# Fused attention and feed-forward kernel: the quantised stage's two maxima by matrix product, its row factors computed inside the rotary block, its first unit by quarters

## The reference, cut to what matters

```python
x = x + _L0_xattn_ref(_layernorm(x), ctx, ctx, ...)      # rotary attention, out @ Wo
x = x + _L0_ffn_ref(_layernorm(x), clip_x, clip_down, w_gate, w_up, w_down)

def _act_fake_quant(x, clip_factor):
    scale = sigmoid(clip_factor) * max(abs(x)) / 127      # ONE scale for the whole tensor
    return clip(round(x / scale), -128, 127) * scale
def _weight_fake_quant(w):                                # one scale for each row
    scale = max(abs(w), axis=1) / 127
    return clip(round(w / scale), -128, 127) * scale
xq = _act_fake_quant(x, clip_x)
gate, up = xq @ wq(w_gate).T, xq @ wq(w_up).T             # 512 -> 1408
h = _act_fake_quant(silu(gate) * up, clip_down)
return h @ wq(w_down).T
```

## Time and profile before

| | us |
|---|---|
| median of 3 timed executions | 1569.18 |
| lowest and highest | 1568.81, 1569.34 |
| span of the profiled execution | 1565.3 |
| PE busy | 1471.0 (94%) |
| DVE busy | 1184.2 (76%) |
| ACT busy | 881.9 (56%) |
| POOL busy | 489.1 (31%) |

### The profile page before, as it was taken

How to read it: one execution, slowest core, us unless ns; L and a number is a source line. 1 busy time by engine, 2 the same in 40 slices (tenths; PEclk the granted TensorE clock), 3 DMA queues, 4 the chain that set the end, 5 groups by cost and what they waited for, 6 DMA issues and landing times. The chain is left out here.

```text
span 1565.3 us, 30701 instructions
## 1 busy us (share of the span) xinstructions
PE 1471.0 (94%) x10998; PEld 1078.9 (69%) x11022; DVE 1184.2 (76%) x2306; ACT 881.9 (56%) x2093; POOL 489.1 (31%) x436
## 2 busy tenths in 40 slices
PE   7899999999999999599998998999999977998997
PEld 5677777777777777444443467888888866776885
DVE  5677777886777655478878968888888756787875
ACT  3444444444444443456657838888988865664342
POOL 0122222222222221200002544545545434664333
PEclk9999999999999999799999999999999998999998
DMA  8411111110111101113304810000000007225641
GB/s 308 153 45 44 44 44 44 44 40 8 43 34 34 43 8 75 44 75 148 148 1 178 324 40 3 4 2 2 3 4 3 4 1 269 82 82 182 205 151 60
DMA packets 47808, 118.35 MB, mean 76 GB/s; under 512 B 9422, under 2 KB 15950, under 8 KB 46032
## 3 DMA queue, kind: packets, MB, share of 16 engines
q1 hardware_dynamic: 42016, 100.03, 18.1%
q0 software_dynamic: 5680, 16.85, 2.7%
HBM read 78.89 MB, written 39.80 MB: 76 GB/s over the span
## 5 line engine op out<-in xcount | busy, mean ns | idle before, releaser
L1721 ACT ACTIVATE c_probs<-c_score,c_minus_top 128x128 f32<-128x128 f32 x512 | 183.8, 422 | 2.0 <-DVE c_minus_top L1833 2.0
L1676 POOL TENSOR_TENSOR c_probs<-c_probs,c_recip 128x1024 f32<-128x1024 f32 x64 | 121.7, 1902 | 169.7 <-DVE c_recip L1839 169.7
L689 POOL TENSOR_TENSOR a_attn_lo_parts<-a_attn,a_attn_hi_parts 128x512 fp32r<-128x512 f32 x64 | 80.1, 1285 | 250.2 <-ACT a_attn_hi_parts L747 250.2
L1721 ACT ACTIVATION_READ_ACCUMULATOR c_probs<-c_score,c_minus_top 128x1 f32 x512 | 133.9, 262 | 0.0
L743 ACT COPY a_attn<-a_pv_ps 128x512 f32<-128x512 f32 x64 | 37.0, 578 | 162.7 <-PE a_pv_ps L998 162.6
L425 PE MATMUL a_bank<-a_x_hi_parts,a_wq_hi 128*128 128x256 f32 x512 | 106.8, 290 | 0.3 <-PEq L440 0.3
L2287 ACT CAST d_xT_hi<-d_turn 128x512 fp32r<-128x512 f32 x71 | 41.7, 587 | 110.1 <-PE d_turn L2531 103.1
L425 PE MATMUL a_bank<-a_x_lo_parts,a_wq_hi 128*128 128x256 f32 x512 | 103.0, 283 | 0.0
L425 PE MATMUL a_bank<-a_x_hi_parts,a_wq_lo 128*128 128x256 f32 x512 | 102.8, 282 | 0.0
L966 PE MATMUL a_bank<-a_wo_hi,a_attn_hi_parts 128*128 128x512 f32 x256 | 102.4, 400 | 0.0
L967 PE MATMUL a_bank<-a_wo_lo,a_attn_hi_parts 128*128 128x512 f32 x256 | 101.1, 395 | 0.0
(11 more groups left out here) (310 smaller groups left out, 4276.0 us busy)
## 6 DMA issues: line engine op xcount, KB each, us to landing
hidden<-b_hidden SPq DMA_DIRECT2D x5, 2816.0 KB, 8.1
b_hidden<-hidden SPq DMA_DIRECT2D x5, 2816.0 KB, 11.9
xres<-in_x SPq DMA_DIRECT2D x8, 1024.0 KB, 14.0
d_we<-in_we SPq DMA_DIRECT2D x8, 1024.0 KB, 12.7
xres<-in_w_gate_up SPq DMA_DIRECT2D x7, 1024.0 KB, 5.3
d_got<-rows SPq DMA_DIRECT2D x20, 258.0 KB, 2.9
xres<-rows SPq DMA_DIRECT2D x19, 258.0 KB, 2.9
a_rot<-in_rot SPq DMA_DIRECT2D x16, 256.0 KB, 3.1
```

The lines of the kernel that those rows point to most:

```text
L689: nc.gpsimd.tensor_tensor(of_spread(attn_lo, g), of_spread(attn, g), of_spread(attn_hi, g), ALU.subtract).then_inc(attn_lo_ready, 1)
L1676: nc.gpsimd.tensor_tensor(part, part, recip[:, t % 2, heads].unsqueeze(2).to_broadcast([P, HALF, KEYS]), ALU.mult).then_inc(scaled, 1)
L1721: last = nc.scalar.activation(probs[:, t, at, :], score_ps[:, h, g, :], ACT.Exp, bias=minus_top[:, h, g:g + 1], accum_out=total[:, t, at:a ...
```

## The change

1. **Both maxima by a product.** POOL's two reductions over partitions go. PE multiplies the column of 128 partition maxima, broadcast as the stationary operand, with the identity (one fp32 product of 128 columns). Each partition then holds all 128 values in PSUM, and DVE reduces them.
2. **Row factors inside the rotary block.** `center` of the last two tiles, the power, the sigmoid, the first maximum and the chain behind it move from the quantised stage's first block to the end of the rotary block. The sigmoid's two instructions come behind the aggregation of the first 30 tiles.
3. **Weights turned elsewhere.** 6 groups ahead of `output(0)` instead of 9, none of them waiting for ACT; the other 6 behind `output(1)`, still in the rotary block. ACT loads Silu's table ahead of its seventh copy. `output(0)` starts when two of the four low parts are there, and waits for the other two at its fifth block.
4. **Rows turned tile by tile.** In the first chunk PE turns tile t as soon as it is rounded, and ACT copies it.
5. **First unit by quarters.** Behind each tile but the first PE issues the gate and up products of the previous tile's 128 rows for unit 0; the usual loop leaves unit 0 out.
6. **Down weights.** SP no longer waits for the turned groups in this stage.

```diff
-    GROUPS_AHEAD = 9
+    GROUPS_AHEAD = 6
@@ rotary block, POOL, behind chunks(pool, body)
+                pool.wait_ge(ahead.var_ready, 2)
+                late = ahead.rstd[:, TILES - NT:]
+                nc.gpsimd.tensor_tensor(late, late, minus_half[:], ALU.pow).then_inc(ahead.rstd_ready, 1)
@@ ACT
-                for g in range(ahead.GROUPS_AHEAD):
+                for g in range(len(ahead.GROUPS)):
+                    if g == ahead.GROUPS_AHEAD:
+                        nc.scalar.activation(warm[:], minus_half[:, 0:1], ACT.Silu)
                     act.wait_ge(ahead.turned, g + 1)
@@ DVE, behind chunks(dve, body)
+                dve.wait_ge(ahead.seen_here, 2 * NT)
+                seen.center(nc, ahead_steps, ahead, slice(TILES - NT, TILES))
+                dve.wait_ge(ahead.rstd_ready, 2)
...
+                nc.vector.tensor_reduce(peak, seen.top[:], AX.X, ALU.max).then_inc(ahead.peak_ready, 1)
+                dve.wait_ge(ahead.peak_turned, 1)
+                ahead_steps.step(nc.vector.tensor_reduce(x_scale, peak_bank[:, 0, 0:P], AX.X, ALU.max))
...
+                nc.vector.scalar_tensor_tensor(ahead.shift[:], ahead.mv[:, :, 0], -1.0, ahead.rstd[:], ALU.mult, ALU.mult)
+                nc.vector.tensor_scalar(ahead.scale[:, 0:2 * IT], ahead.scale[:, 0:2 * IT], x_scale, None, ALU.mult)
@@ PE, output(t), and behind chunks(pe, body)
-                            pe.wait_ge(attn_lo_ready, UNITS * n)
+                            pe.wait_ge(attn_lo_ready, UNITS * n - 2)
...
+                            if t == 0 and k == BLOCKS // 2:
+                                pe.wait_ge(attn_lo_ready, UNITS * n)
...
+                for g in range(ahead.GROUPS_AHEAD, len(ahead.GROUPS)):
+                    pe.wait_ge(ahead.taken, g - len(turn_places) + 1)
+                    ahead.turn(nc, g, turn_places[g % len(turn_places)])
+                pe.wait_ge(ahead.peak_ready, 1)
+                pe.wait_ge(freed["dve"], last_out.emptied[1])
+                nc.tensor.matmul(peak_bank[:, 0, 0:P], row_scale[:, 0:1].to_broadcast([P, P]), ident[:], start=True, stop=True).then_inc(ahead.peak_turned, 1)
@@ quantised stage, first block, SP, POOL, ACT
-                    sp.wait_ge(ahead.turned, groups)
-                    nc.gpsimd.partition_all_reduce(peak_all[:], peak[:], P, bass.bass_isa.ReduceOp.max).then_inc(peak_all_ready, 1)
+                    def take_first(t):
+                        act.wait_ge(x_full, t + 1)
+                        nc.scalar.copy(xT[:, 0, :, t * P:(t + 1) * P], bank[:, t % 2, 0:D].rearrange("p (k c) -> p k c", k=KB)).then_inc(x_freed, 1)
                     for t in range(TPC):
                         scale_rows(0, t)
-                    for k in range(KB):
-                        take_turned(0, k)
+                        if t >= 2:
+                            take_first(t - 2)
+                    for t in range(TPC - 2, TPC):
+                        take_first(t)
@@ PE
-                    pe.wait_ge(x_quant, TPC)
-                    for k in range(KB):
-                        turn(0, k)
-                    pe.wait_ge(ahead.taken, groups)
+                    def turn_first(t):
+                        pe.wait_ge(x_quant, t + 1)
+                        if t >= 2:
+                            pe.wait_ge(x_freed, t - 1)
+                        for k in range(KB):
+                            last = nc.tensor.transpose(bank[:, t % 2, k * P:(k + 1) * P], whole_x[:, t, k * P:(k + 1) * P], ahead.ident[:])
+                        last.then_inc(x_full, 1)
+                    def first_quarter(t):
+                        pe.wait_ge(x_freed, t + 1)
+                        tokens = slice(t * P, (t + 1) * P)
+                        for ps, w, full in ((gate_ps, gateT, gate_full), (up_ps, upT, up_full)):
+                            for k in range(KB):
+                                last = nc.tensor.matmul(ps[:, 0, tokens], w[:, k, 0:P], xT[:, 0, k, tokens], start=(k == 0), stop=(k == KB - 1))
+                            if t == TPC - 1:
+                                last.then_inc(full, 1)
+                    turn_first(0)
+                    for t in range(1, TPC):
+                        turn_first(t)
+                        first_quarter(t - 1)
+                    first_quarter(TPC - 1)
@@ second block, POOL, DVE, PE
-                    nc.gpsimd.partition_all_reduce(peak_all[:], peak[:], P, bass.bass_isa.ReduceOp.max).then_inc(peak_all_ready, 1)
+                    dve.wait_ge(peak_turned, 1)
+                    ch.step(nc.vector.tensor_reduce(peak_all[:], out_ps[:, BANKS - 1, 0:P], AX.X, ALU.max))
+                    pe.wait_ge(peak_ready, 1)
+                    nc.tensor.matmul(out_ps[:, BANKS - 1, 0:P], peak[:].to_broadcast([P, P]), ident[:], start=True, stop=True).then_inc(peak_turned, 1)
```

More of the change, by code:

```diff
@@ L305, in rope_attention_stage @@
         row_scale, row_inv = sb("row_scale", [P, 4]), sb("row_inv", [P, 4])
+        warm = sb("warm", [P, 1])
         score_ps = pb("score_ps", [P, 2, 4, ROPE_CHUNK])
@@ L620, in rope_attention_stage @@
         turn_places = [score_banks[:, i, :] for i in range(4)] + [x[:].rearrange("p a c -> p (a c)").bitcast(BF16) for x in (pv_ps, sum_ps)]
+        last_out = ring.use(NC, 0, plan(NC)["O0"])
+        peak_bank = last_out.out
         def of_spread(x, g):
@@ L902, in body @@
                         seen.center(nc, ahead_steps, ahead, slice(0, TILES - NT))
-                        ahead.steps = ahead_steps.k
+                        dve.wait_ge(ahead.sig_exp, 1)
+                        ahead_steps.step(nc.vector.tensor_scalar(ahead.clip[:], ahead.sigm[:], 1.0, None, ALU.add))
+                        ahead_steps.wait()
+                        ahead_steps.step(nc.vector.reciprocal(ahead.sigm[:], ahead.clip[:]))
                     first = isinstance(n, int) and n == 0
@@ L1055, in body @@
                         for g in range(ahead.GROUPS_AHEAD):
-                            if g >= len(turn_places):
-                                pe.wait_ge(ahead.taken, g - len(turn_places) + 1)
-                            ahead.turn(nc, g, turn_places[g % len(turn_places)])
+                            ahead.turn(nc, g, turn_places[g])
                     if "O0" in s:
@@ L1148, in quantised_ffn_stage @@
             h_seen = sem("h_seen")
-            half_ready, shift_ready, scales_ready = sem("half_ready"), sem("shift_ready"), sem("scales_ready")
             down_turned, down_taken = sem("down_turned"), sem("down_taken")
-            first_group, groups = ahead.GROUPS_AHEAD, len(ahead.GROUPS)
-            turn_places = [gate_ps[:, g, :].bitcast(BF16) for g in range(groups - first_group)]
             DOWN_GROUPS = -(-IT // 2)
@@ L1183, in scale_rows @@
                         tile = n * TPC + t
-                        if tile == 0:
-                            act.wait_ge(shift_ready, 1)
                         if tile >= 2:
@@ L1198, in take_down @@
                         nc.scalar.copy(downT[:, 2 * g:2 * g + len(down_columns(g)), :].rearrange("p i d -> p (i d)"), bank[:, g % 2, 0:n]).then_inc(down_taken, 1)
-                    for g, place in enumerate(turn_places):
-                        act.wait_ge(ahead.turned, first_group + g + 1)
-                        ahead.take(nc, first_group + g, place).then_inc(ahead.taken, 1)
-                    act.wait_ge(half_ready, 1)
-                    nc.scalar.activation(silu[:, 0, 0:1], spare[:, 0:1], ACT.Silu)
+                    def take_first(t):
+                        act.wait_ge(x_full, t + 1)
+                        nc.scalar.copy(xT[:, 0, :, t * P:(t + 1) * P], bank[:, t % 2, 0:D].rearrange("p (k c) -> p k c", k=KB)).then_inc(x_freed, 1)
                     for t in range(TPC):
                         scale_rows(0, t)
-                    for k in range(KB):
-                        take_turned(0, k)
+                        if t >= 2:
+                            take_first(t - 2)
+                    for t in range(TPC - 2, TPC):
+                        take_first(t)
                     for n in range(CHUNKS):
@@ L1299, in turn_down @@
                         last.then_inc(down_turned, 1)
-                    for g, place in enumerate(turn_places):
-                        ahead.turn(nc, first_group + g, place)
-                    pe.wait_ge(x_quant, TPC)
-                    for k in range(KB):
-                        turn(0, k)
-                    pe.wait_ge(ahead.taken, groups)
+                    def turn_first(t):
[18 more added lines that the diff above has]
+                    first_quarter(TPC - 1)
                     for n in range(CHUNKS):
-                        pe.wait_ge(x_freed, KB * (n + 1))
+                        if n >= 1:
+                            pe.wait_ge(x_freed, KB * (n + 1))
                         for i in range(IT):
                             u = n * IT + i
```

(2 more changed lines are left out.)

59 lines of the change are left out of this document (18 added, 41 removed).

## The result

| | before | changed |
|---|---|---|
| median of the timed runs beside each other | 1569.26 us (1568.81 to 1571.52, 4 runs) | 1554.41 us (1552.98 to 1555.43, 4 runs) |
| ratio, 95% interval | | 0.9896 [0.9881, 0.9911] |
| profiled execution: span, its own time | 1565.3, 1567.1 | 1553.5, 1555.43 |

Faster: by 1.0% by the ratio, and the medians lie 14.9 us apart. (1567.1 is no reading of the execution profiled before: it is its span plus the 1.8 that 45 other executions of that kernel show between span and time, 1.72 to 1.86; see e8.)

The account below looks back on a forecast made before the run. PE, busy for 94% of the span, bounds most stretches; at the touched seams all engines wait for one chain. Terms -2.9 - 6.3 + 0.15 - 3.2 + 0.3 = -11.95 took 1569.2 to 1557.2 us, range 1555.4 to 1560.0.

Parts of the forecast that it names:

- Six groups ahead: End of the rotary stage: fewer weight transposes ahead of output tile 0 let it start earlier, -2.9 us.
- The first maximum: Chain behind the rotary stage: a product and DVE reduction taking 0.8 replace the 7.08 around POOL's reduction, -6.3 us.
- The block's end: End of the rotary block: ACT goes on only after the weight scales, not once the shifts are there, +0.15 us.
- A: Stretch from POOL's first low part to ACT's first scaling, terms -9.05; E ends at POOL's first masked-stage instruction.
- The quarters: First chunk of the quantised stage: turning tile by tile and unit 0 by quarters bring the second hidden unit earlier, -3.2 us.
- T: The moment ACT begins scaling the first rows in the quantised stage, forecast to move from 658.45 to 649.4.
- The second maximum: Second seam, inside the quantised stage: the product costs 0.8 where the POOL reduction cost 0.49, +0.3 us.
- The sum against the time: Step from profiled span to timed median: the median's 3.9 us above the span was carried over unchanged.
- Quarters give little: Rival, first chunk: PE stays at 1.2 GHz through unit 1 or ACT's copies come late; 1558.4 to 1559, chance 0.18.
- Output tile 0 held: Rival, end of rotary stage: output tile 0 still waits for POOL's fourth part; 2.2 lost, 1559.4, chance 0.05.
- The stall moves: Rival: a later POOL instruction on the last stage's path pays the 6.7 us stall; 1563.9, chance 0.05.
- Slower: Rival: the clock stays at 1.2 GHz in the first chunk; 1573.7 if all ten later units are slow, chance 0.02.

Follow-up runs that it names:

- e8: The kernel before, run again unchanged for a second profiled execution: 1566.83 us, ratio 0.9999.
- e10: The changed kernel with nine groups of down weights turned ahead again and one wait for all low parts: 1558.21 us, ratio 0.9943.
- e6_all: The changed kernel with output tile 0 waiting for all four low parts at once, without the split wait: 1560.16 us, ratio 0.9926.
- e11: The changed kernel with the second maximum by POOL's reduction again, plus an unused POOL reduction in the quantised stage's first block: 1554.73 us.
- e6_unused: The changed kernel plus one unused POOL reduction in the first block of the quantised stage: 1555.5 us, ratio 0.9909.
- e4: The changed kernel, run again unaltered for a second trace: 1556.42 us, ratio 0.9913.
- e1: The kernel before with only the two POOL reductions replaced by the product and DVE's reduction, in their old places: 1561.92 us, ratio 0.9948.
- e2: The kernel before plus one unused POOL reduction at its start: 1569.33 us, ratio 0.9997.
- e7: The changed kernel plus 26, 24 and 28 unused identity products on PE around the first maximum and first turning: 1554.81 us, ratio 0.9899.
- e9: The changed kernel plus unused identity products at the first seam and 50 more behind the second maximum's product: 1556.29 us, ratio 0.9927.

## Why the prediction was wrong

Its mechanisms held, nearly to the number. Of the 2.8 between the forecast and 1554.41, 0.9 are terms, nearly all of it the quarters; the rest is the step from the sum to the forecast, which took single executions for fixed quantities and gave the range none of their scatter.

- **Six groups ahead, -2.9:** right. -2.94 at output tile 0, e10 gives 2.98 back. No wait at the fifth block, with the 0.6 of slack that I had worked out; without it e6_all pays 2.3 (I had 2.2). POOL's and ACT's covers held. (The idle 10.46 of rows 3 stood ahead of ACT's tenth group, not its seventh; ahead of the seventh the table load and 5.55 of idle time found room.)
- **The first maximum, -6.3:** right within 0.15, against the execution that was profiled; against e8's it would have been -4.6, so the closeness is in part luck. 7.08 became 0.91; I had 0.8. The product is 0.49 at full clock and not 0.28: I read the 276 ns of one record, of a product with 32 weight columns, and this one leaves two records. My reserve for a lone product covered half of it.
- **The block's end, +0.15:** +0.12 (0.3 and 0.11 later behind the chain, 0.29 earlier in front of it). A as a whole: -9.16 against -9.05; the 0.17 beyond these three terms are output tiles 0.10 and a chain on DVE 0.07 shorter.
- **The quarters, -3.2:** undersized by 0.9. I had taken the middle between 2.8 and 3.7 because I didn't know when in T + 5.7 to T + 9.2 the clock would return. It returned at T + 6.4, and the last quarter was done by T + 7.0, not 7.5, so that all of unit 1 ran at 2.4 GHz. Second hidden unit: T + 9.03 measured, T + 9.4 to 10.3 forecast. How much of it comes hangs on the clock's return: in the variants that leave this stretch alone the clock was back at T + 5.4 (e6_all), 6.6 (e10), 7.5 (e11) and 7.9 (e6_unused), and the second unit at T + 8.87, 9.07, 9.37 and 9.57. So the term is worth 3.5 to 4.3 against the first trace's 13.12, and even with the late clock more than I took.
- **The second maximum, +0.3:** +0.42 where it stands, again the product's 0.49, but not to be seen at the stage's end (e11), where the traces differ by as much among themselves.
- **The sum against the time: the failed step.** "The median of the timed runs is 3.9 above the span, and I leave that as it is." It is not a quantity that can be left. 1.8 of it lie outside the span (1.72 to 1.86 in each of the 45 executions of the kernel before that ran beside these kernels); the other 2.1 are the distance between the execution that was profiled and the three that were timed (1568.81 to 1569.34), draws from a scatter of 6 us. From the execution in which the durations were read, the same sum gives 1565.3 + 1.8 - 11.95 = 1555.15, still 0.2 below the range's low end but 0.7 from the measured median; with the terms as measured (-12.8) it gives 1554.3. That this base hits 1554.41 is itself luck of the draw. The changed kernel's ten timed executions (four with the result, six in e4) run from 1552.23 to 1558.63 with a median of 1555.05, and my base with the measured terms gives 1556.4, which is e4's median. The medians of before beside these kernels run from 1566.83 (e8) to 1570.62 (e1's group), so no base of one or three executions is good to better than some 2 us. What is left of the 14.9 beyond the 12.05 to 13.55 that the traces have from A to E is not traced to any instruction.
- **The range** was built of the terms' bounds alone, and took three runs within 0.5 us as the kernel's scatter. With 3 us to either side for that scatter it would have held the result.
- **The rivals.** "Quarters give little": no, they gave more. "Output tile 0 held": no, but exact as to price (e6_all). "The stall moves": its premise, a cost of the first use, fell with e2; no later POOL instruction pays it in the changed kernel, which has no such reduction left. "Slower": the clock was back at 654.4.
- **The prices of the product and of the stall.** The product shows two records and 0.49, the stall 5.6 to 8.8 in these runs. "FP8 and Floating Point Precision" of the Trainium skill ("TensorE Precision Notes") has 4 passes for true FP32; what the product does inside a record no trace here shows, but the page's direction was right: by it the sum was to be 0.2 to 0.3 worse over both maxima, and the product took 0.21 more than the row that I read, twice. "GPSIMD Engine Reference" of the Trainium skill ("Instruction dispatch") has about 6 us for the first call to a freshly loaded kernel. The size agrees roughly (5.58 to 8.77); that it comes again at a later call of the same execution (e2) the page doesn't say, and the runs do.

## What to carry to other kernels

A profiled span and a median of three timed runs are both draws: take the base of a forecast from as many executions as there are, and give the range their scatter even where the few shown lie close. A POOL reduction over partitions on a serial chain costs its 0.4 us only if POOL has done nothing else since the last one; a product of the maxima with the identity and a reduction on DVE took 0.91 at full clock, 1.2 at half, where PE was free. At a seam, cut the first unit of the next product so that PE starts with the first tile that is ready: it saves the waiting, and gives the clock time to return before the dense work.

## What the runs showed of the hardware that was not expected

- The wait ahead of POOL's reduction came back when POOL had run tensor instructions in between (8.77, then 7.63 in one execution of e2), each time behind a pair of MODIFY_POOL_CONFIG records, and differed between executions of one kernel (7.12 and 5.58); with POOL idle in between, for 165 us (e11) and 178 (before), there was none.
- An fp32 product of 128 columns with 128 x 128 weights takes 0.49 at full clock and 0.80 at half, as a pair of records.
- 78 small products that nothing uses, laid into PE's idle time, kept its granted clock at 1.00 through a seam of some 10 us (e7); at the next seam 50 more halved the time at half clock and bought nothing, since PE waits for DVE's rounding there (e9).
- Half clock appears in some executions and not in others at the same place of the same work, in stretches where PE is busy too, and spans of 1.56 ms that differ by up to 6 us go with it: about 0.4 us for each us of half clock in the masked stage, (380.1 - 377.5) over 7 more us.
